# Destination numbers and attribute rows of two neighbouring ring slots in one transfer each, and the node bases of four supertiles in one register load

## The reference, cut to what matters

```
for l in range(3):
    h_in = h
    hx = h @ W_node[l]
    ef = relu(edge_attr @ W_e1[l] + b_e1[l]) @ W_e2[l] + b_e2[l]
    xi = hx[dst]
    xj = hx[src]
    att_in = concatenate([xi, xj, edge_attr], axis=-1)
    a = sigmoid(relu(att_in @ Wa1[l] + ba1[l]) @ Wa2[l] + ba2[l])
    msg = a * (xj + ef)
    out = segment_sum(msg, dst, num_segments=n) + bias[l]
    out = layer_norm(out, ln_g[l], ln_b[l])
    if l < 2: out = relu(out)
    h = out + h_in
```

## Time and profile before

| | us |
|---|---|
| median of three timed runs | 12152.69 |
| lowest, highest | 12151.59, 12154.09 |
| the profiled execution: first to last instruction | 14505.9 |
| in it, POOL busy | 9098.4 (63%) |
| PE busy | 6046.6 (42%) |
| DVE busy | 5160.3 (36%) |
| ACT busy | 2253.6 (16%) |

### The profile page before, as it was taken

The page is one execution under the profiler, slowest core; times in us unless marked ns, Lnnn a source line. Parts: engine busy times, 40 slices in busy tenths (PEclk is TensorE's granted clock), DMA queues, the critical chain, the costliest instruction groups (busy, mean ns, idle before and its releaser), DMA issues.

```text
span 14505.9 us, 188761 instructions
## 1 busy us (share of the span) xinstructions
PE 6046.6 (42%) x29601; PEld 5317.3 (37%) x29602; DVE 5160.3 (36%) x15464; ACT 2253.6 (16%) x6488; POOL 9098.4 (63%) x9456
## 2 busy tenths in 40 slices
PE   4344444444444434444444444443444444344444
PEld 3333333333333333333333333333333333333333
DVE  4333333333333333333333333333333333333333
ACT  1111111111111111111111111111111111111111
POOL 5666666666666566666666666656666666666665
DMA  5222222222222222222222222222222222222222
GB/s 142 65 66 66 67 66 67 67 67 67 66 66 67 63 64 66 67 66 67 66 67 65 66 67 66 67 63 64 65 66 66 65 66 65 65 66 66 65 66 62
DMA packets 922293, 981.09 MB, mean 68 GB/s; under 512 B 496648, under 2 KB 769578, under 8 KB 921881
## 3 DMA queue, kind: packets, MB, share of 16 engines
q0 software_dynamic: 300000, 615.00, 17.0%
q1 hardware_dynamic: 512652, 324.11, 8.4%
q10 hardware_dynamic: 109611, 41.70, 1.1%
HBM read 928.45 MB, written 51.36 MB: 68 GB/s over the span
## 4 chain that ended last, share of the span: by engine, by line
SPq 53%; issue 43%; DVE 1%; another core or an unknown queue 1%; PE 1%; POOL 1%; DVEq 0%; DMA 0%; ACT 0%; ACTq 0%; POOLq 0%
SPq L472 19%; SPq L487 12%; SPq L468 8%; SPq L469 8%; SPq L488 2%; SPq L309 2%; POOL msg_all L553 0%; SPq L424 0%; PE zr_ps L786 0%; PE out_ps L793 0%; PE zr_ps L773 0%; DMA left<-attr_parts 0%; DVE plow L931 0%; DVEq L1055 0%
## 5 line engine op out<-in xcount | busy, mean ns | idle before, releaser
L553 POOL DMA_INDIRECT msg_all<-gather_table,idx x9375 | 9022.0, 962 | 5278.7 <-issue 2617.9
L793 PE MATMUL out_ps<-ahot,msg_all 128*128 128x32 f32 x18750 | 4382.7, 403 | 2352.7 <-issue 1308.6
L793 PEld LDWEIGHTS out_ps<-ahot,msg_all 128*128 128x128 f32 x18750 | 4142.3, 329 | 2827.2 <-issue 2251.0
L786 PE MATMUL zr_ps<-right,left 117*128 117x128 bf16 x9375 | 1305.6, 304 | 5558.5 <-DVE left L1018 2951.4
L786 PEld LDWEIGHTS zr_ps<-right,left 117*128 117x128 bf16 x9375 | 890.3, 135 | 5754.7 <-issue 5751.6
L679 ACT ACTIVATE msg_all<-zr_ps 128x320 f32<-128x320 f32 x1875 | 819.2, 437 | 11231.1 <-remote 6786.3
L1018 DVE TENSOR_SCALAR left<-rel,pidx 96x640 bf16<-96x640 int16 x1875 | 770.8, 411 | 4441.8 <-DMA left<-attr_parts 2701.9
L1024 DVE TENSOR_TENSOR z<-zr_ps,msg_all 128x320 f32<-128x320 f32 x1875 | 908.3, 484 | 1084.9 <-DMA msg_all<-gather_table,idx 508.4
L1059 DVE TENSOR_TENSOR acc<-acc,out_ps 128x32 f32 x1875 | 354.0, 189 | 2440.7 <-issue 1168.7
L1044 DVE TENSOR_REDUCE logit<-zw 128x5 f32<-128x320 f32 x1875 | 895.3, 477 | 168.7 <-issue 157.1
L1037 DVE SCALAR_TENSOR_TENSOR zw<-z,cur 128x320 f32<-128x320 f32 x1875 | 908.5, 485 | 126.5 <-issue 125.2
(11 more groups left out here) (113 smaller groups left out, 1289.1 us busy)
## 6 DMA issues: line engine op xcount, KB each, us to landing
rel<-dst_minus_base SPq DMA_DIRECT2D x1875, 120.0 KB
msg_all<-gather_table,idx POOLq DMA_INDIRECT x9375
right<-p_table SPq DMA_DIRECT2D x1875, 12.0 KB
left<-attr_parts SPq DMA_DIRECT2D x1875, 11.2 KB
left<-attr_parts SPq DMA_DIRECT2D x1875, 7.5 KB
left<-attr_parts SPq DMA_DIRECT2D x1875, 3.8 KB
gather_table<-tabs ACTq DMA_DIRECT2D x98, 128.0 KB, 1.8
p_table<-pparts ACTq DMA_DIRECT2D x98, 96.0 KB, 2.3
```

Of the source, the lines that this page charges most:

```text
L553: pool.indirect_dma_start(out=msg[k][:, j, 0:2 * C], out_offset=None, in_=table, in_offset=bass.IndirectOffsetOnAxis(ap=idx[:, k, j:j + 1] ...
L786: t = pe.matmul(zr_tile(par, j), left[k][0:K, j * P:(j + 1) * P], right[0:K, k, :], start=True, stop=True)
L793: t = pe.matmul(out_ps[:, par, 0:WIN], msg[k][:, j, C:3 * C], ahot[:, par, j, :], start=(j == 0), stop=(j == TILES - 1))
```

## The change

The four buffers `rel0` to `rel3` become one tensor `rel_ring`, the four `left` buffers one tensor `left_ring`, with the slots side by side. SP now works at slots 0 and 2 only. There it waits until the later one of two neighbouring slots is free, and issues for both supertiles together: one transfer of destination numbers twice as wide, two transfers of window rows (their places in the table differ), and three transfers of attribute rows twice as wide. The node bases of a round are read at slot 0 by one load instruction into four registers. The supertile left over at a layer's end is loaded alone. One semaphore for each pair of slots takes the place of one for each slot, so both DVE and PE wait for the transfers of the whole pair.

```diff
-        rel = [sb(f"rel{k}", [PICK, EDGES], I16) for k in range(SLOTS)]
-        left = [sb(f"left{k}", [P, EDGES], BF16) for k in range(SLOTS)]
+        rel_ring = sb("rel_ring", [PICK, SLOTS * EDGES], I16)
+        rel = [rel_ring[:, k * EDGES:(k + 1) * EDGES] for k in range(SLOTS)]
+        left_ring = sb("left_ring", [P, SLOTS * EDGES], BF16)
+        left = [left_ring[:, k * EDGES:(k + 1) * EDGES] for k in range(SLOTS)]
...
+        def pair_landed(l, i, k):
+            p = k // PAIR
+            whole = ROUNDS * PAIR_LOADS + (LOADS if p == 0 else 0)
+            alone = isinstance(i, int) and i == ROUNDS
+            return l * whole + i * PAIR_LOADS + (LOADS if alone else PAIR_LOADS)
...
-                def loads(s, k, p_row, landed):
-                    sp.dma_start(rel[k][:, :], rel_d[bass.ds(s, 1), :].to_broadcast([PICK, EDGES])).then_inc(landed, 16)
-                    sp.dma_start(right[0:PICK, k, 0:C], ptable[bass.ds(p_row, WIN)].rearrange("n t c -> (n t) c")).then_inc(landed, 16)
+                def loads(s, k, p_rows, landed):
+                    width = len(p_rows) * EDGES
+                    ring = slice(k * EDGES, k * EDGES + width)
+                    sp.dma_start(rel_ring[:, ring], rel_row[:, bass.ds(s * EDGES, width)].to_broadcast([PICK, width])).then_inc(landed, 16)
+                    for n, p_row in enumerate(p_rows):
+                        sp.dma_start(right[0:PICK, k + n, 0:C], ptable[bass.ds(p_row, WIN)].rearrange("n t c -> (n t) c")).then_inc(landed, 16)
                     at = PICK
                     for parts in range(PARTS, 0, -1):
-                        sp.dma_start(left[k][at:at + parts * A, :],
-                                     attr_rows[0:parts * A, bass.ds(s * EDGES, EDGES)]).then_inc(landed, 16)
+                        sp.dma_start(left_ring[at:at + parts * A, ring],
+                                     attr_rows[0:parts * A, bass.ds(s * EDGES, width)]).then_inc(landed, 16)
...
                 def step(i, s, k):
-                    base = sp.value_load(base_i[0:1, bass.ds(s, 1)], min_val=0, max_val=N - 1)
-                    sp.wait_ge(s_zr, freed(l, s, SLOTS))
-                    loads(s, k, nc.s_assert_within(base + l * NPAD, 0, L * NPAD - WIN), s_ld[k])
+                    alone = isinstance(i, int) and i == ROUNDS
+                    if k % PAIR:
+                        return
+                    if k == 0:
+                        _, bases = nc.values_load_multi_w_load_instructions(
+                            base_i[0:1, bass.ds(s, 1 if alone else SLOTS)], engines=[mybir.EngineType.SP],
+                            min_val=0, max_val=N - 1)
+                        round_rows[:] = [nc.s_assert_within(base + l * NPAD, 0, L * NPAD - WIN) for base in bases]
+                    width = 1 if alone else PAIR
+                    sp.wait_ge(s_zr, freed(l, s + width - 1, SLOTS))
+                    loads(s, k, round_rows[k:k + width], s_ld[k // PAIR])
...
-                    pe.wait_ge(s_ld[k], (uses(l, i, k) + 1) * LOADS)
+                    pe.wait_ge(s_ld[k // PAIR], pair_landed(l, i, k))
...
-                    dve.wait_ge(s_ld[k], (uses(l, i, k) + 1) * LOADS)
+                    dve.wait_ge(s_ld[k // PAIR], pair_landed(l, i, k))
```

More of the change, by code:

```diff
@@ L46 @@
 AHEAD = SLOTS - 1
+PAIR = 2
 GB = 7
@@ L215, in gnn_kernel @@
         s_gat = [sem(f"gathered{k}") for k in range(SLOTS)]
-        s_ld = [sem(f"edge_loads_landed{k}") for k in range(SLOTS)]
+        s_ld = [sem(f"edge_pair_loads_landed{p}") for p in range(SLOTS // PAIR)]
         s_pick = sem("pick_ready")
@@ L260, in gnn_kernel @@
         LOADS = 16 * (2 + PARTS)
+        PAIR_LOADS = 16 * (1 + PAIR + PARTS)
         IN_DMAS = 4 + SLOTS + 2 + 2 * TERMS + PARTS
@@ L465, in _ @@
                 attr_rows = attr_d.rearrange("t (a e) -> (t a) e", a=A)
-                def loads(s, k, p_row, landed):
-                    sp.dma_start(rel[k][:, :], rel_d[bass.ds(s, 1), :].to_broadcast([PICK, EDGES])).then_inc(landed, 16)
-                    sp.dma_start(right[0:PICK, k, 0:C], ptable[bass.ds(p_row, WIN)].rearrange("n t c -> (n t) c")).then_inc(landed, 16)
+                rel_row = rel_d.rearrange("(o s) n -> o (s n)", o=1)
+                def loads(s, k, p_rows, landed):
[4 more added lines that the diff above has]
+                        sp.dma_start(right[0:PICK, k + n, 0:C], ptable[bass.ds(p_row, WIN)].rearrange("n t c -> (n t) c")).then_inc(landed, 16)
                     at = PICK
                     for parts in range(PARTS, 0, -1):
-                        sp.dma_start(left[k][at:at + parts * A, :],
-                                     attr_rows[0:parts * A, bass.ds(s * EDGES, EDGES)]).then_inc(landed, 16)
+                        sp.dma_start(left_ring[at:at + parts * A, ring],
+                                     attr_rows[0:parts * A, bass.ds(s * EDGES, width)]).then_inc(landed, 16)
                         at += parts * A
@@ L479, in window @@
                     row_ = nc.s_assert_within(node + v * WIN + l * NPAD, 0, L * NPAD - WIN)
-                    loads(s, 0, row_, s_bd)
+                    loads(s, 0, [row_], s_bd)
                 beyond(sp, l, window)
@@ L483, in _ @@
                 mark(sp)
+                round_rows = []
                 def step(i, s, k):
-                    base = sp.value_load(base_i[0:1, bass.ds(s, 1)], min_val=0, max_val=N - 1)
-                    sp.wait_ge(s_zr, freed(l, s, SLOTS))
-                    loads(s, k, nc.s_assert_within(base + l * NPAD, 0, L * NPAD - WIN), s_ld[k])
+                    alone = isinstance(i, int) and i == ROUNDS
[9 more added lines that the diff above has]
+                    loads(s, k, round_rows[k:k + width], s_ld[k // PAIR])
                 supertiles(sp, [(0, step)])
```

## The result

Where the change was first timed, it takes 12124.21 us (median of 10 runs, 12119.21 to 12130.52) against 12153.81 for the kernel before (10 runs, 12151.59 to 12155.47): a ratio of 0.9976, interval 0.9968 to 0.9984, 29.6 us or 0.24% faster. The experiments timed it three times more, each time beside the kernel before on the same chip, and there it is slower: 1.0016 (1.0007 to 1.0025), 1.0009 (1.0000 to 1.0018) and 1.0009 (1.0000 to 1.0018). Both have to be explained.

The account below looks back on a forecast made before the run. The prediction took POOL's own gather pace, not SP, to bound the timed kernel. Its terms, 0 + 0 + 0 + 0, left the time at 12153 us, with an 8-in-10 range of 12085 to 12215.

Parts of the forecast that it names:

- POOL's sum: All that POOL alone must take, mainly 9375 gathers at 1.2507 us: 12137.9 us, 14.8 us under the timed median.
- 140.6 us of lengthening: Term of POOL's sum for gathers longer than the median: (962 - 947) ns x 9375.
- Fewer transfers: On SP, 3744 fewer transfers save about 1.9 ms of SP time, covered by POOL's gathers: 0 on the path.
- the later wait: SP's loads of s start 6.3 us later; 12.3 us remain against a need of 4.7: cost 0.
- two slots on one semaphore: The pick of s also waits for rows of s+1, counted in the 4.7 us need: nothing of note.
- the likeliest case: POOL's pace kept, a change under 0.2% (24 us), 12129 to 12177 us; chance 0.49.
- Same bytes in other bunches: SP's regrouped loads may shift gather landings and reach POOL: taken as 0, bounds -141 to +84 us.
- the edge: Where `ahot` starts just ahead of or behind the third gather; 0.08 us in landing turns 0.12 us on or off.
- The mechanism at POOL: `ahot` starting just ahead of a gather lengthens it by 0.12 us, 1.9% of a supertile.
- SP's traffic at the landing: Every second landing would meet a double set of SP's loads and the others none; no size given for the shift.
- Which way: Direction in which bunched loads shift the landing against the edge: no row showed it; faster 0.24, same 0.49, slower 0.27.
- edge rival: Landings move off the edge (12083 or 12012 us, chance 0.23) or onto it (12195 or 12237 us, chance 0.25).

Follow-up runs that it names:

- changed_again: The changed kernel itself, timed again beside the kernel before on the same chip: 12129.3 us against 12108.0, ratio 1.0016.
- before_again: The kernel before, unchanged, timed and profiled again on the same chip as its own comparison runs: 12108.4 us against 12108.0, ratio 1.0000.
- the fourth set: Its step alone: the kernel before with `z_sum`'s gather wait count computed from its own terms, SP untouched: 12164.6 us against 12138.4, ratio 1.0022.
- loads_after_landing: The kernel before with one more SP wait, so loads of s also wait for `z_sum` of s-4: 12113.6 us against 12108.0, ratio 1.0002.
- the changed kernel with its chain earlier: The changed kernel with `z_sum` over four of five tiles, the fifth tile's sum left out: 12108.9 us against 12121.5 for the kernel before.
- changed_ahot_after_logits: The changed kernel with DVE's logits put ahead of hot_times_a, so `ahot` starts later: 11981.8 us against 12116.0 for the kernel before.
- changed_beside: The changed kernel itself, timed beside the kernel before on the fourth set's chip: 12148.6 us against 12138.4, ratio 1.0009.

## Why the prediction was right and wrong

- *What bounds the kernel.* Right, and confirmed directly: POOL's sum gave 12137.9 where the profile pointed at SP; re-profiled, the kernel before has a span of 12105.6 and 12119.8 us, no gather waits for SP, and one register load for four changed nothing. There is luck in how well the sum came out: its 140.6 us of lengthening was read from the long execution, in which `z_sum` starts over 3.5 us after the last gather's end in 1371 supertiles of 1875. In the two undisturbed profiles the same term is 128 and 135 us.
- *Fewer transfers, the later wait, two slots on one semaphore: 0.* Right. 5631 transfers and 471 reads as counted; the idle time before gathers is the same, 2923 against 2925 us.
- *The predicted time.* 12153 against 12124 lies within the range, but the likeliest case, no change, does not hold for the first comparison: it was off by 29 us where 24 was its bound. The other three comparisons (+10, +10, +21) are within the 24.
- *The step that failed* is the term "Same bytes in other bunches", put at 0 because "the mean over landings scattered on both sides of the edge hardly moves". The mean moves: side by side, changed_again has 23.6 us more gather time than before_again. And what moved it had been passed over in the sentence "The wait counts on DVE and PE are computed in registers before and after; nothing of note." In two slots of four `z_sum` starts 0.07 us earlier, and the fourth set shows that this step alone is worth 26 us.
- *The mechanism at POOL* was right: 0.12 us of a gather hang on the place of `ahot`, and moving `ahot` proved it. It was only half of the matter. In before_again the gathers held under `ahot` cost 67 us, those under `window_pick` and `z_weighted` 23 and 26, which the prediction did not look for.
- *SP's traffic at the landing* was right in kind: the late landings now fall in every second supertile and are nearly absent from the others, as predicted. It gave no size for the delay, which is about 1 us, and it expected the delay to decide the time; taking all of it away changed nothing (loads_after_landing).
- *Which way.* Each edge rival was true somewhere. Why the first comparison came out at -30 us stays open. Two things differ there. In the changed kernel's first profile the packets land at 1.18 us, 0.06 earlier than in any other trace; in the first profile of the kernel before they land at 1.24, in the 356 supertiles where this can be read. So the nearest counterpart is the changed kernel with its chain earlier beside the kernel before untouched, and that is -12.6 us. And the gathers of the two first profiles have other medians (947 and 945 ns); the same kernel shows both values, so this is nothing of the kernels' doing, and it is 19 us over 9375 gathers. Together that makes an estimate of -32 us, from one profile of each kernel, one of them disturbed. A side-by-side in which packets land early would tell, and none was had.

## What to carry to other kernels

A profiled execution can be bound by something the timed runs don't have: before believing the chain, add up the busiest engine's own pace and compare it with the timed median. When one engine's instructions stand in a fixed place against another's, a single wait instruction more or less can change how often they collide; look for the collision itself and move it well away, here by exchanging two stages in DVE's order, which was worth 115 to 134 us (0.9904 and 0.9888) where the change under study was worth 10 to 30 of either sign. A median can also hide a second group: the table of landings looks the same for all kernels until the late ones, a quarter to a third of them in most kernels here, are counted by slot. And a difference of 0.2% between two kernels may belong to the set of runs as much as to the kernel, until it has been seen in a second set.

## What was not expected of the hardware

- A gather is held by `ahot`, a DVE instruction with two SBUF inputs, when that starts just ahead of it. With `ahot` 0.18 to 0.21 us ahead the gather takes 0.947 us, with 0.12 to 0.15 ahead 0.999, 0.09 to 0.12 ahead 1.032, 0.03 to 0.06 ahead 1.091, and from 0.02 on 0.944 again (means in before_again). The rise is one for one: the gather is held until 0.19 us after the start of `ahot`, 0.13 before its end. The Trainium skill (SBUF — State Buffer, on port contention) has the later of the two blocked until the first ends. The trace agrees with the one-for-one rise, but not with the full length, and not in the other order: in changed_ahot_after_logits `ahot` starts 1868 times within a running gather and still takes 0.316 us.
- Other DVE instructions do the same: in before_again all gathers that start 0.03 to 0.15 us behind `zw` (52, mean 1.228 us) and 56 of 57 behind `hot` are held. Behind `z_sum`, which has one input in PSUM, and behind the reduction `logit`, with one input, 1 of 120 and 0 of 137 are.
- A landing comes about 1 us later (last packet at 2.27 us in the median, otherwise 1.25) when SP starts its loads in the 0.3 us ahead of the end of the supertile's last gather: 306 of 307 in before_again, 340 of 340 in changed_again.
- Two ways of writing one wait count, with the same value, differ by a wait instruction of DVE and by 26 us in 12138.
- The median gather is 944 to 945 ns in most profiles and 947 in others, on one chip too: changed_beside took 12124.84 us in its profiled execution, at a median of 944, and 12140.66 to 12151.98 in its ten others; the three other profiles on that chip have 947.
